# Layer 2 of a two-layer graph network: squares, adds, the last group's scores and the scaling of P in another order and on another engine

## The chip, the cores and the metric

The kernel runs on 1 core of one Trainium2 chip. The time is device microseconds of one execution, from start to end, the median of three runs. Each core has TensorE (PE, matrix products), VectorE (DVE), ScalarE (ACT), GpSimd (POOL) and SyncE (SP, which here issues DMA transfers). The engines run their own instruction streams and meet only at semaphores.

## What is computed

128 graphs of 64 nodes with 384 features go through two attention layers. The second, which the change touches, is this one, with `x` the output of the first:

```python
def _L1_gnn_ref(x, spatial_encoding, edge_encoding, Wq, Wk, Wv, bv, Wo, bo):
    scale = jnp.asarray(HIDDEN, x.dtype) ** (-0.5)
    q = (x @ Wq.T).reshape(b, n, NUM_HEADS, HEAD)          # 12 heads of 32
    k = (x @ Wk.T).reshape(b, n, NUM_HEADS, HEAD)
    v = (x @ Wv.T + bv).reshape(b, n, NUM_HEADS, HEAD)
    bias = (spatial_encoding + edge_encoding)[:, None]     # twice adj
    scores = jnp.einsum('bqhd,bkhd->bhqk', q, k) * scale + bias
    row_nonzero = jnp.any(scores != 0, axis=-1, keepdims=True)
    scores = jnp.where(row_nonzero, scores, -jnp.inf)
    p = jnp.nan_to_num(jax.nn.softmax(scores, axis=-1))
    out = jnp.einsum('bhqk,bkhd->bqhd', p, v).reshape(b, n, h)
    return out @ Wo.T + bo
...
x = _layernorm(x + _L1_gnn_ref(x, adj, adj, ...), axis=-1)
```

## The kernel before

The 8192 rows (nodes) are cut into 32 groups of 256, each of 2 tiles of 128 rows. Layer 1 takes the first 1386 us of the span, layer 2 the rest; layer 2 has one function `step(g, ...)` per engine, written out for groups 0 and 1, run in a hardware loop for g = 2 to 30, and written out again for g = 31 (no more groups), 32 (back half alone) and 33 (squares and norm alone). There is no planner: each engine's order is the order of the calls in its `step`. The three steps of a group overlap: in step g the front half (V, scores, softmax) works on group g, the back half (P^T, PV, output projection, y) on b = g - 1, and the late part (layer norm) on g - 2. Q and K of group g + 1 are made in step g as well.

Precision: the dense products are made of three matmuls each, high and low parts of both operands (`mm3`), so activations are split into `xt_hi`/`xt_lo` and `ctxt_hi`/`ctxt_lo`: ScalarE writes the high part, VectorE subtracts it for the low part.

The order on each engine in a loop step:

- TensorE: `values(g, 0)` (V of tile 0, 9 matmuls), `turn_p` of both tiles of b (12 transposes into the banks `two`, which are the same PSUM as the scores' `four`), `values(g, 1)`, `wait_for_pv` (copies of P^T done, V rows swapped and kept, ctx's low part read), `scores(g)` (96 small matmuls), `pv` (96), `qk(g + 1)` in three banks (54), `attn_out(b)` (18). `turn_p` waits for the scaled P of its tile and for y of the group before (which reads the same banks).
- ScalarE: `square` twice, `take_pt` twice (P^T out of PSUM), `xt_high` (behind both tiles of V), `ctxt_high` twice (behind PV), `keep_v` (four copies), `norm` twice, then `take_q` three times with `exp` of tile 0 and 1 between them.
- VectorE: `take_v` twice, `xt_low`, `ctxt_low(b, 0)`, `add_adj` twice (scores plus adj, PSUM to SBUF), `find_max` twice, `ctxt_low(b, 1)`, per tile `find_magnitude` and `invert_sum` (sum, reciprocal, mask), then `finish(b)`: y = projection + residual for both tiles, and the mean.
- GpSimd: `root(g - 2)` (three small operations behind the squares), `shift` of both tiles (score minus maximum, into P), `scale_p` of both tiles (P times the reciprocal of its sum).
- SyncE: loads of x^T, the residual and adj, four swaps of V rows, and the store of the normed group.

Lines of the trace (a helper's line may stand for several places): L1423 is `mm3`; L1461 the scores; L1469 the transposes of P; L1488 PV; L1543 `xt_high`; L1549 `take_q`; L1557 and L1558 `keep_v`; L1562 `exp`; L1567 `take_pt`; L1574 `ctxt_high`; L1580 `square`; L1587 `norm`; L1636 `xt_low`; L1645 `take_v`; L1655 `add_adj`; L1663 `find_max`; L1670 `find_magnitude`; L1676, L1679, L1682 the sum, reciprocal and mask of `invert_sum`; L1689 `ctxt_low`; L1699 to L1703 `finish`; L1746 `shift`; L1753 `scale_p`; L1758 to L1762 `root`. L953 is layer 1's own subtraction of the maximum, on VectorE.

Of the kernel before, what the change touches and what calls it, by code (L numbers as in the profile page):

```python
# [26 lines left out]
ALU = mybir.AluOpType  # L27
# [3 lines left out]
P = 128  # L31
GRAPHS, NODES, D = 128, 64, 384
TOKENS = GRAPHS * NODES
TILES = 2
# [4 lines left out]
H0, H1 = 8, 12  # L39
# [1276 lines left out]
def layer1(nc, block, sem, x2, x2T, adj, out, shared, last, free):  # L1316
# [5 lines left out]
    with ExitStack() as ctx:  # L1322
# [21 lines left out]
        score, prob, pt = (sb(f"b_{n}", [P, TILES, S]) for n in ("score", "p", "pt"))  # L1344
# [74 lines left out]
        def _(pe):  # L1419
# [88 lines left out]
            def step(g, front=True, back=True, more=True):  # L1508
                b = g - 1
                if front:  # L1510
                    values(g, 0)
                if back:
                    for t in range(TILES):
                        turn_p(b, t)
                if front:
                    values(g, 1)
                if back:
                    wait_for_pv(b)
                if front:
                    scores(g, back)  # L1520
                if back:
                    for t in range(TILES):
                        pv(b, t)
                if front and more:
                    for u in range(3):
                        qk(g + 1, u)
                if back:
                    for t in range(TILES):
                        attn_out(b, t, front)
# [3 lines left out]
            with pe.Fori(2, NG - 1) as g:  # L1533
                step(g)
# [4 lines left out]
        def _(act):  # L1539
# [54 lines left out]

            def step(g, front=True, back=True, late=True, more=True):
                b = g - 1
                if late:
                    for t in range(TILES):
                        square(g - 2, t)
                if back:  # L1600
                    for t in range(TILES):
                        take_pt(b, t)
                if front and more:
                    xt_high(g + 1)
                if back:
                    for r in range(2):
                        ctxt_high(b, r)
                if front:
                    for t in range(TILES):
                        keep_v(g, t)  # L1610
                if late:
                    norm(g - 2)
                if front and more:
                    take_q(g + 1, 0)
                if front:
                    exp(g, 0)
                if front and more:
                    take_q(g + 1, 1)
                if front:
                    exp(g, 1)  # L1620
                if front and more:
                    take_q(g + 1, 2)
# [10 lines left out]
        def _(dve):  # L1633
# [38 lines left out]
            def invert_sum(g, t):  # L1672
# [9 lines left out]
                dve.scalar_tensor_tensor(out=rden[:, t, :], in0=samax[:, t, :], scalar=0.0, in1=rden[:, t, :],  # L1682
                                         op0=ALU.is_gt, op1=ALU.mult).then_inc(rden_masked, 1)

            def ctxt_low(g, r):
                dve.wait_ge(ctxt_hi, 2 * g + r + 1)
                for low, high, k in CTX_ROWS[r]:
                    at = (k - r) * GROUP
                    i = dve.tensor_tensor(ctx_t[1][low:high, k, :], one[PV_BANK[r]][low:high, at:at + GROUP],  # L1689
                                          ctx_t[0][low:high, k, :].bitcast(F32), ALU.subtract)  # L1690
                i.then_inc(ctxt_lo, 1)
# [15 lines left out]

            def step(g, front=True, back=True, late=True, more=True):
                b = g - 1
                if front:  # L1710
                    for t in range(TILES):
                        take_v(g, t)
                if front and more:
                    xt_low(g + 1)
                if back:
                    ctxt_low(b, 0)
                if front:
                    for t in range(TILES):
                        add_adj(g, t)
                    for t in range(TILES):  # L1720
                        find_max(g, t)
                if back:
                    ctxt_low(b, 1)
                if front:
                    for t in range(TILES):
                        find_magnitude(g, t)
                        invert_sum(g, t)
                if back:
                    finish(b)

# [9 lines left out]
        def _(pool):  # L1740
# [5 lines left out]
                pool.tensor_tensor(p, s, smax[:, t, :].unsqueeze(2).broadcast_to([P, H1, NODES]),  # L1746
                                   ALU.subtract).then_inc(shifted, 1)

            def scale_p(g, t):

                s = prob[:, t, :].rearrange("p (h n) -> p h n", h=H1)
                pool.wait_ge(rden_masked, TILES * g + t + 1)
                pool.tensor_tensor(s, s, rden[:, t, :].unsqueeze(2).broadcast_to([P, H1, NODES]), ALU.mult).then_inc(p_scaled, 1)  # L1753

            def root(g):

                pool.wait_ge(sq_done, TILES * (g + 1))
# [6 lines left out]
            def step(g, front=True, back=True, late=True, more=True):  # L1764
                if front and not back:
                    last["gpsimd"]()
                if late:
                    root(g - 2)
                if front:
                    for t in range(TILES):  # L1770
                        shift(g, t)
                    for t in range(TILES):
                        scale_p(g, t)

            step(0, back=False, late=False)
            step(1, late=False)
# [87 lines left out]
```

## Time and profile before

| what | value |
|---|---|
| median of 3 runs | 1971.73 us (1971.13 to 1973.51) |
| the profiled execution | 1973.86 us |
| its span, first to last instruction | 1972.0 us |
| PE, PEld (weight loads) busy | 95%, 93% |
| DVE busy | 66% |
| ACT busy | 55% |
| POOL busy | 25% |
| granted TensorE clock, mean | 0.98 |

Busy shares are means over both layers. Starts in the rows below are microseconds from the start of the span; a row of the timeline is start, duration, engine, line, operation, output<-inputs, shapes, and in brackets the idle time of the engine before it and what ended it. Several like instructions are merged into one row with their count (x2, x96). Recorded ends of neighbours on one engine overlap a little, so distances are best read from start to start.

### The profile page before, as it was taken

Reading aid. Unit: us, or ns where it says so; the run is one execution under the profiler, and the core shown is the slowest. Engines: PE = TensorE matmul, PEld = TensorE weight load, DVE = VectorE, ACT = ScalarE, POOL = GpSimd, SP = SyncE. Lnnn points to the kernel's source line nnn. Section 1 sums busy time; section 2 is a strip of 40 time slices with the busy share of each in tenths; the row PEclk is TensorE's granted clock in tenths of the full one; section 3 lists DMA queues with packets and bytes.
Section 4 is the critical chain, followed back from the end, with each engine's and each line's share of the span. In section 5 each row is a group of like instructions: output and inputs, shape, how many; then the busy total and the mean of one; then the engine's idle time right before and its main releaser. Section 6 shows DMA issues by size and latency. Waiting matters only on the chain.

```text
span 1972.0 us, 58076 instructions
## 1 busy us (share of the span) xinstructions
PE 1870.0 (95%) x22160; PEld 1830.5 (93%) x22160; DVE 1291.8 (66%) x2507; ACT 1081.0 (55%) x2366; POOL 496.2 (25%) x616
## 2 busy tenths in 40 slices
PE   7699999999999999999999999988799999999996
PEld 6599999999999999999999999988789999999995
DVE  5566666666666666666666666654577777777775
ACT  4365455654556545655556555544456656565654
POOL 0111122121221112121131211211333344433343
PEclk8899999999999999999999999999899999999998
DMA  7534444444444444444444444334322233222231
GB/s 184 150 105 113 126 119 113 127 109 128 116 119 120 112 129 115 124 118 109 135 109 123 117 113 132 99 98 106 84 80 71 84 88 88 80 81 76 85 88 59
DMA packets 268682, 213.42 MB, mean 108 GB/s; under 512 B 142816, under 2 KB 251104, under 8 KB 268640
## 3 DMA queue, kind: packets, MB, share of 16 engines
q1 hardware_dynamic: 268640, 212.85, 39.6%
q8 instruction: 28, 0.46, 0.1%
q14 instruction: 14, 0.11, 0.0%
HBM read 120.33 MB, written 79.69 MB: 101 GB/s over the span
## 4 chain that ended last, share of the span: by engine, by line
PE 83%; ACT 5%; DVE 4%; DMA 3%; SPq 3%; issue 2%; POOL 0%; ACTq 0%; DVEq 0%; POOLq 0%
PE a_bank L446 29%; PE a_banks L446 28%; PE b_bank L1423 12%; PE b_banks L1423 5%; PE a_bank L495 2%; ACT b_pt L1567 2%; PE b_banks L1461 2%; PE b_bank L1488 2%; PE a_banks L515 2%; SPq L262 1%; PE b_banks L1469 1%; ACT b_unused L1580 1%; DMA a_work<-x_turned 1%; DMA x_turned<-a_work 0%; DMA a_work<-ctx_turned 0%
## 5 line engine op out<-in xcount | busy, mean ns | idle before, releaser
L446 PE MATMUL a_bank<-a_x1t_hi,a_w_hi 128*128 128x256 f32 x1152 | 328.2, 285 | 20.1 <-DVE a_x1t_lo L917 20.1
L446 PE MATMUL a_bank<-a_x1t_hi,a_w_lo 128*128 128x256 f32 x1152 | 324.7, 282 | 0.0
L446 PE MATMUL a_bank<-a_x1t_lo,a_w_hi 128*128 128x256 f32 x1152 | 324.6, 282 | 0.0
L734 ACT ACTIVATE a_work<-a_bank,a_b 128x256 f32<-128x256 f32 x384 | 160.2, 468 | 203.4 <-PE a_bank L446 202.9
L446 PE MATMUL a_banks<-a_w_hi,a_hid_hi 128*128 128x384 f32 x768 | 258.8, 337 | 0.6 <-DVE a_hid_lo L932 0.6
L446 PE MATMUL a_banks<-a_w_hi,a_hid_lo 128*128 128x384 f32 x768 | 258.2, 336 | 0.0
L446 PE MATMUL a_banks<-a_w_lo,a_hid_hi 128*128 128x384 f32 x768 | 258.2, 336 | 0.0
L932 DVE TENSOR_TENSOR a_hid_lo<-a_work,a_hid_hi 128x512 fp32r<-128x512 f32 x192 | 131.6, 698 | 191.1 <-ACT a_hid_hi L739 191.1
L446 PEld LDWEIGHTS a_bank<-a_x1t_hi,a_w_hi 128*128 128x128 f32 x1152 | 221.0, 192 | 22.9 <-DVE a_x1t_lo L917 21.0
L446 PEld LDWEIGHTS a_bank<-a_x1t_lo,a_w_hi 128*128 128x128 f32 x1152 | 221.6, 192 | 0.0
L446 PEld LDWEIGHTS a_bank<-a_x1t_hi,a_w_lo 128*128 128x128 f32 x1152 | 220.5, 191 | 0.0
L1253 POOL TENSOR_TENSOR a_ms<-a_ssq,eps_rms 128x2 f32<-128x2 f32 x64 | 12.5, 195 | 641.7 <-ACT a_work L744 641.7
L1746 POOL TENSOR_TENSOR b_p<-b_score,b_smax 128x768 f32<-128x768 f32 x64 | 93.1, 1475 | 232.0 <-DVE b_smax L1663 232.0
L446 PEld LDWEIGHTS a_banks<-a_w_hi,a_hid_hi 128*128 128x128 f32 x768 | 144.4, 188 | 1.0 <-DVE a_hid_lo L932 1.0
L446 PEld LDWEIGHTS a_banks<-a_w_hi,a_hid_lo 128*128 128x128 f32 x768 | 144.5, 188 | 0.0
L446 PEld LDWEIGHTS a_banks<-a_w_lo,a_hid_hi 128*128 128x128 f32 x768 | 144.3, 188 | 0.0
L721 ACT ACTIVATE a_x1t_hi<-a_work 128x768 fp32r<-128x768 f32 x32 | 27.1, 847 | 211.2 <-DMA a_work<-x_turned 211.2
L739 ACT ACTIVATE a_hid_hi<-a_work 128x512 fp32r<-128x512 f32 x192 | 121.5, 633 | 8.2
L1753 POOL TENSOR_TENSOR b_p<-b_p,b_rden 128x768 f32<-128x768 f32 x64 | 94.3, 1474 | 56.7 <-DVE b_rden L1682 56.7
L1253 POOL TENSOR_TENSOR a_ms<-a_ssq,eps_ln 128x2 f32<-128x2 f32 x32 | 6.5, 203 | 405.3 <-ACT a_work L744 405.3
L926 DVE TENSOR_TENSOR a_work<-a_banks,a_bv 128x384 f32<-128x384 f32 x64 | 35.6, 558 | 106.6 <-PE a_banks L446 106.4
L1580 ACT ACTIVATE b_unused<-b_y,b_nmean_c 128x384 f32<-128x384 f32 x64 | 38.9, 611 | 112.4 <-DVE b_nmean_c L1703 112.4
(172 smaller groups left out, 5615.2 us busy)
## 6 DMA issues: line engine op xcount, KB each, us to landing
a_work<-in_x SPq DMA_DIRECT2D x64, 384.0 KB, 3.3
p_turned<-a_work SPq DMA_DIRECT2D x256, 64.0 KB, 2.3
a_work<-p_turned SPq DMA_DIRECT2D x32, 512.0 KB, 3.3
xt_raw<-in_xT SPq DMA_DIRECT2D x32, 384.0 KB, 3.9
ctx_turned<-a_work SPq DMA_DIRECT2D x256, 48.0 KB, 1.7
a_work<-ctx_turned SPq DMA_DIRECT2D x32, 384.0 KB, 3.5
x_turned<-a_work SPq DMA_DIRECT2D x256, 48.0 KB, 1.7
a_work<-x_turned SPq DMA_DIRECT2D x32, 384.0 KB, 3.8
```

Source lines behind the costliest of these rows:

```text
L446: r = pe.matmul(out, lhs[a], rhs[b], start=first and n == 0, stop=last and n == 2)
L495: r = pe.matmul(PV_BANK[t][64 * s:64 * s + 64, h * 2 * VW:(h + 1) * 2 * VW].rearrange("p (r c) -> p r c", r=2), pt[:, t, s * 256 + h * 64: ...
L515: r = pe.matmul(s_banks[64 * s:64 * s + 64, i, at:at + n * NODES].rearrange("p (e n) -> p e n", e=n), q[row, m, nodes], k_t[row, m:m + n, ...
L734: r = act.activation(silu[:, p % 2, s * GROUP:(s + 1) * GROUP], A[p % 3][:, s * GROUP:(s + 1) * GROUP], ACT.Silu, bias=b1[:, m:m + 1])
L739: act.activation(hid[0][:, p % RING, :], silu[:, p % 2, :], ACT.Copy).then_inc(hid_hi, 1)
L932: dve.tensor_tensor(hid[1][:, p % RING, :], silu[:, p % 2, :], hid[0][:, p % RING, :].bitcast(F32), ALU.subtract).then_inc(hid_lo, 1)
L1423: r = pe.matmul(out, lhs[a], rhs[b], start=first and n == 0, stop=last and n == 2)
L1461: r = pe.matmul(four[64 * s:64 * s + 64, i, at:at + NODES], qk_t[row, k, nodes], qk_t[row, KT + k, nodes], start=True, stop=True, skip_gro ...
L1488: m = pe.matmul(one[PV_BANK[r]][32 * i:32 * i + 32, at:at + NODES], v_rows[rows, n, h * DH1:(h + 1) * DH1], pt[rows, t, h * P + 64 * s:h * ...
L1580: act.activation(unused[:, t, :], y[:, t, :], ACT.Square, bias=nmean_c[:, t:t + 1], scale=ROOT, accum_out=ssq[:, t:t + 1]).then_inc(sq_don ...
L1746: pool.tensor_tensor(p, s, smax[:, t, :].unsqueeze(2).broadcast_to([P, H1, NODES]), ALU.subtract).then_inc(shifted, 1)
L1753: pool.tensor_tensor(s, s, rden[:, t, :].unsqueeze(2).broadcast_to([P, H1, NODES]), ALU.mult).then_inc(p_scaled, 1)
```

## The change

All of it is in layer 2.

- ScalarE, loop step: the two squares of g - 2 move from the head of the step to behind `take_pt` and `xt_high`, ahead of `ctxt_high`; in the step that has no front half they come behind `ctxt_high`.
- VectorE, loop step: both `add_adj` move ahead of `ctxt_low(b, 0)`. `scale_p` moves from GpSimd to VectorE, behind `invert_sum` of its tile, with the same waits and the same semaphore.
- Group 31 (`front and not more`) gets an order of its own on TensorE, ScalarE and VectorE: TensorE makes its scores ahead of V's second tile and ahead of the transposes of group 30, with waits for y of the group before and for the adds; ScalarE does squares, norm and copies first and puts the exponentials between the halves of ctx's high part; VectorE takes the adds and maxima ahead of V's second tile.

```diff
--- before.py
+++ after.py
@@ -1509,14 +1509,19 @@
                 b = g - 1
                 if front:
                     values(g, 0)
+                if front and not more:
+                    pe.wait_ge(y_done, TILES * b)
+                    scores(g, back)
+                    values(g, 1)
+                    pe.wait_ge(biased, TILES * (g + 1))
                 if back:
                     for t in range(TILES):
                         turn_p(b, t)
-                if front:
+                if front and more:
                     values(g, 1)
                 if back:
                     wait_for_pv(b)
-                if front:
+                if front and more:
                     scores(g, back)
                 if back:
                     for t in range(TILES):
@@ -1594,17 +1599,32 @@
 
             def step(g, front=True, back=True, late=True, more=True):
                 b = g - 1
-                if late:
+                if front and not more:
                     for t in range(TILES):
                         square(g - 2, t)
+                    norm(g - 2)
+                    for t in range(TILES):
+                        take_pt(b, t)
+                    for t in range(TILES):
+                        exp(g, t)
+                        ctxt_high(b, t)
+                    for t in range(TILES):
+                        keep_v(g, t)
+                    return
                 if back:
                     for t in range(TILES):
                         take_pt(b, t)
                 if front and more:
                     xt_high(g + 1)
+                if front and late:
+                    for t in range(TILES):
+                        square(g - 2, t)
                 if back:
                     for r in range(2):
                         ctxt_high(b, r)
+                if late and not front:
+                    for t in range(TILES):
+                        square(g - 2, t)
                 if front:
                     for t in range(TILES):
                         keep_v(g, t)
@@ -1682,6 +1702,12 @@
                 dve.scalar_tensor_tensor(out=rden[:, t, :], in0=samax[:, t, :], scalar=0.0, in1=rden[:, t, :],
                                          op0=ALU.is_gt, op1=ALU.mult).then_inc(rden_masked, 1)
 
+            def scale_p(g, t):
+
+                s = prob[:, t, :].rearrange("p (h n) -> p h n", h=H1)
+                dve.wait_ge(rden_masked, TILES * g + t + 1)
+                dve.tensor_tensor(s, s, rden[:, t, :].unsqueeze(2).broadcast_to([P, H1, NODES]), ALU.mult).then_inc(p_scaled, 1)
+
             def ctxt_low(g, r):
                 dve.wait_ge(ctxt_hi, 2 * g + r + 1)
                 for low, high, k in CTX_ROWS[r]:
@@ -1707,17 +1733,35 @@
 
             def step(g, front=True, back=True, late=True, more=True):
                 b = g - 1
+                if front and not more:
+                    take_v(g, 0)
+                    for t in range(TILES):
+                        add_adj(g, t)
+                    for t in range(TILES):
+                        find_max(g, t)
+                    find_magnitude(g, 0)
+                    take_v(g, 1)
+                    invert_sum(g, 0)
+                    scale_p(g, 0)
+                    for r in range(2):
+                        ctxt_low(b, r)
+                    find_magnitude(g, 1)
+                    invert_sum(g, 1)
+                    scale_p(g, 1)
+                    finish(b)
+                    return
                 if front:
                     for t in range(TILES):
                         take_v(g, t)
                 if front and more:
                     xt_low(g + 1)
+                if front:
+                    for t in range(TILES):
+                        add_adj(g, t)
                 if back:
                     ctxt_low(b, 0)
                 if front:
                     for t in range(TILES):
-                        add_adj(g, t)
-                    for t in range(TILES):
                         find_max(g, t)
                 if back:
                     ctxt_low(b, 1)
@@ -1725,6 +1769,7 @@
                     for t in range(TILES):
                         find_magnitude(g, t)
                         invert_sum(g, t)
+                        scale_p(g, t)
                 if back:
                     finish(b)
 
@@ -1746,12 +1791,6 @@
                 pool.tensor_tensor(p, s, smax[:, t, :].unsqueeze(2).broadcast_to([P, H1, NODES]),
                                    ALU.subtract).then_inc(shifted, 1)
 
-            def scale_p(g, t):
-
-                s = prob[:, t, :].rearrange("p (h n) -> p h n", h=H1)
-                pool.wait_ge(rden_masked, TILES * g + t + 1)
-                pool.tensor_tensor(s, s, rden[:, t, :].unsqueeze(2).broadcast_to([P, H1, NODES]), ALU.mult).then_inc(p_scaled, 1)
-
             def root(g):
 
                 pool.wait_ge(sq_done, TILES * (g + 1))
@@ -1769,8 +1808,6 @@
                 if front:
                     for t in range(TILES):
                         shift(g, t)
-                    for t in range(TILES):
-                        scale_p(g, t)
 
             step(0, back=False, late=False)
             step(1, late=False)
```

## Rows read from the trace of the kernel before

**Rows 1.** Waits of layer 2: engine line <- releaser: us in total, times, longest us

```profile
PE b_banks L1461 <- ACT b_pt L1567: 21.3, 30, 0.8
```

**Rows 2.** Chain of work that ended last, one group: start us, us, what

```profile
1849.10 1.40 ACT b_pt L1567 x2
1850.50 0.43 issue
```

**Rows 3.** Timeline of TensorE in steps 26 and 27

```profile
1847.18 1.49 PE L1469 MATMUL b_banks<-ident,b_p 128*128 128x128 f32 x12
...
1849.89 0.34 PE L1423 MATMUL b_bank<-wv_lo,xt_hi 128*128 128x384 f32 x1
1850.93 1.25 PE L1461 MATMUL b_banks<-b_qk 32*64 32x64 f32 x96 [0.70 <-ACT b_pt L1567]
...
1864.36 0.34 PE L1423 MATMUL b_bank<-wv_lo,xt_hi 128*128 128x384 f32 x1
```

**Rows 4.** Timeline of VectorE: xt_low of groups 1 to 3, then one step

```profile
1414.15 0.96 DVE L1636 TENSOR_TENSOR xt_lo<-xt_raw,xt_hi 128x768 fp32r<-128x768 f32 x1 [0.38 <-ACT xt_hi L1543]
...
1430.84 0.96 DVE L1636 TENSOR_TENSOR xt_lo<-xt_raw,xt_hi 128x768 fp32r<-128x768 f32 x1 [0.34 <-ACT xt_hi L1543]
...
1449.93 0.96 DVE L1636 TENSOR_TENSOR xt_lo<-xt_raw,xt_hi 128x768 fp32r<-128x768 f32 x1 [0.34 <-ACT xt_hi L1543]
...
1851.26 0.96 DVE L1636 TENSOR_TENSOR xt_lo<-xt_raw,xt_hi 128x768 fp32r<-128x768 f32 x1 [0.34 <-ACT xt_hi L1543]
1854.04 0.75 DVE L1689 TENSOR_TENSOR b_ctxt_lo<-b_bank,b_ctxt_hi 128x256 fp32r<-128x256 f32 x2 [1.83 <-ACT b_ctxt_hi L1574]
1854.71 1.80 DVE L1655 TENSOR_TENSOR b_score<-b_banks,b_adj 128x768 f32<-128x768 f32 x2
1856.44 1.80 DVE L1663 TENSOR_REDUCE b_smax<-b_score 128x12 f32<-128x768 f32 x2
1858.27 0.87 DVE L1689 TENSOR_TENSOR b_ctxt_lo<-b_bank,b_ctxt_hi 64x256 fp32r<-64x256 f32 x2
1859.05 0.94 DVE L1670 TENSOR_REDUCE b_samax<-b_score 128x12 f32<-128x768 f32 x1
1859.93 0.95 DVE L1676 TENSOR_REDUCE b_psum<-b_p 128x12 f32<-128x768 f32 x1
...
1861.18 0.17 DVE L1682 SCALAR_TENSOR_TENSOR b_rden<-b_samax,b_rden 128x12 f32<-128x12 f32 x1
1861.26 0.94 DVE L1670 TENSOR_REDUCE b_samax<-b_score 128x12 f32<-128x768 f32 x1
...
1863.56 0.56 DVE L1699 SCALAR_TENSOR_TENSOR b_y<-b_banks,b_res 128x384 f32<-128x384 f32 x1
```

**Rows 5.** Timeline of ScalarE, the same step

```profile
1850.39 0.83 ACT L1543 ACTIVATE xt_hi<-xt_raw 128x768 fp32r<-128x768 f32 x1
1853.36 1.45 ACT L1574 ACTIVATE b_ctxt_hi<-b_bank 128x256 fp32r<-128x256 f32 x4 [2.14 <-PE b_bank L1488]
...
1856.21 1.31 ACT L1587 ACTIVATE b_normed<-b_y,b_ymean,b_rstd 128x384 f32<-128x384 f32 x2
1857.43 0.58 ACT L1549 ACTIVATE b_qk<-b_bank 128x512 f32<-128x512 f32 x1
```

**Rows 6.** Timeline of GpSimd, the same step

```profile
1857.54 2.91 POOL L1746 TENSOR_TENSOR b_p<-b_score,b_smax 128x768 f32<-128x768 f32 x2 [7.12 <-DVE b_smax L1663]
```

**Rows 7.** Timeline of TensorE in step 1, written out, without squares

```profile
1412.84 0.34 PE L1423 MATMUL b_bank<-wv_lo,xt_hi 128*128 128x384 f32 x1
1413.11 1.25 PE L1461 MATMUL b_banks<-b_qk 32*64 32x64 f32 x96
```

**Rows 8.** Line 953, layer 1: duration ns min/median/max, first and last start us

```profile
L953 DVE TENSOR_TENSOR a_work<-a_work,a_smax x64: 691/694/1329, 26.8 to 1280.6; 128x512 f32<-128x512 f32 x64
```

**Rows 9.** Timeline of TensorE, steps 31 and 32

```profile
1934.33 1.49 PE L1469 MATMUL b_banks<-ident,b_p 128*128 128x128 f32 x12
...
1955.29 1.29 PE L1488 MATMUL b_bank<-b_pt,b_v_rows 64*32 64x64 f32 x96 [1.95 <-ACT b_pt L1567]
```

## The prediction

> **What bounds the kernel now.** All edits lie in layer 2, so I read that layer alone. The table of waits names few stalls of TensorE there; the one that returns is 0.7 us ahead of the scores, put down to ScalarE's copy of P^T, 30 times [rows 1]. In the code the two squares stand right ahead of that copy; in the chain of waits of one group the two copies take 1.40 us, and 0.43 us of issue follow ahead of the scores [rows 2]. On TensorE itself the last matmul of V's second tile starts at 1849.89 and the scores at 1850.93, 1.04 us later [rows 3]. Group 1, which has no squares, shows what that step takes without a stall: 1412.84 to 1413.11, 0.27 us [rows 7]. So the stall costs 1.04 - 0.27 = 0.77 us a group. The period is the distance of two starts of xt_low: (1851.26 - 1449.93) / 23 = 17.45 us [rows 4]. TensorE without the stall would need 16.68.
>
> Then I read VectorE against it. From ctx's first low part (1854.04) to the first add of y (1863.56) it has no gap: each instruction starts as the last one ends [rows 4]. So the present ring is: y and its mean on VectorE, squares, copies of P^T, scores and PV, ctx's high part, VectorE's row of work, y again. TensorE is full, but the ring around VectorE is just as long.
>
> **The change part by part.** (a) Squares behind the copies and xt_high. They leave the way to the scores. Two of them cost about the 1.22 us of the equally large pair of norms (1856.21 to 1857.43) [rows 5]. The copies then end about 2.4 us after the transposes start (the second set of six transposes ends near 1.2, 0.4 for the signal, 0.8 for half the pair), and V's second tile has its last matmul 2.71 us after that start (1847.18 to 1849.89) [rows 3]. So the stall of 0.77 goes, if the five waits that follow in TensorE's queue (0.43 us behind the copy today [rows 2]) are passed meanwhile. Their new place is between xt_high (starts 1850.39, some 0.75) and ctx's high part, which waits for PV. Counted from V's last matmul (1849.89): xt_high at 0.50, squares 1.25 to 2.47, ctx's high part at 0.27 + 2.43 (1850.93 to 1853.36) = 2.70 [rows 3, 5]. They fit, with 0.2 to spare. GpSimd's three small operations come later, and norm behind the copies of V still finds them done.
>
> (b) Adds ahead of ctx's low part. VectorE no longer idles for ScalarE after xt_low (1851.26, 0.96 long): the adds follow it at once, since the scores are done by then. The low part (0.67 us, 1854.04 to 1854.71) goes behind them; its only near consumers, the third bank of the next Q/K and the output projection, come over 2 us later. Moved, at no price.
>
> (c) P scaled on VectorE. GpSimd's multiply goes (same width as its subtraction, 2.91 / 2 = 1.46 us [rows 6]); VectorE gets two of 128x768 with both inputs in SBUF. The nearest row is xt_low, 0.96 busy, 0.89 to the next start after the overlap seen between neighbours [rows 4]. The other row is layer 1's subtraction with the same broadcast, 0.69 for 512 columns at best, which gives 0.69 x 768 / 512 = 1.04 at most, and 1.33 at worst [rows 8]. I take 0.89; ends 0.85 and 1.04. Twice 0.89 plus 0.13 of waiting for each mask (0.21 in place of 0.08, an estimate from the mask's own length) is 2.0 us more on VectorE each group. This lies on the ring, because y is added behind it.
>
> VectorE's two-input multiply can collide with GpSimd. Layer 1's row shows the same instruction at 0.69 at best and 1.33 at worst [rows 8], though nothing about its own size varies. The Trainium skill (SBUF — State Buffer, Who interferes with whom) says that a VectorE instruction with two SBUF inputs and a GpSimd instruction that reads SBUF shut each other out for a whole instruction. By that rule the multiply is safe only where GpSimd rests; with it the sum would be the rival "collision" below, otherwise it stays as it is.
>
> (d) The new ring. From the start of xt_low: xt_low 0.89, adds 1.73 (1854.71 to 1856.44), low part 0.67, maxima 1.83 (to 1858.27), second low part 0.78, magnitude 0.88, sum to mask 1.25 (1859.93 to 1861.18), mask 0.21, multiply 0.89; then for tile 1 magnitude 0.88, 1.25, 0.21, 0.89; y 0.56 [rows 4]. That is 12.92. Then the wake of TensorE, an estimate of 0.15 (ends 0 and the 0.43 of rows 2), transposes and V to its last matmul 2.71 [rows 3], to xt_high 0.50, to xt_low 0.87 (1850.39 to 1851.26) [rows 4, 5]. Sum 17.15.
>
> Does the first sum find its exponential? By GpSimd: maxima start at 3.29, the subtraction follows 1.10 later as today (1856.44 to 1857.54), and 2.39 behind its start VectorE sums (to 1859.93) [rows 4, 6]: 3.29 + 1.10 + 2.39 = 6.78, just when VectorE is free (6.78). By ScalarE's queue, from V's last matmul: 0.27 + 2.43 to ctx's high part, 2.85 to norm, 1.22 to take_q, 0.58 to the exponential (its copy 0.5 to 0.58), 0.88 to the sum (2.39 less 1.46 of subtraction and 0.05 of signal), 8.2, less 1.37 for the start of xt_low: 6.85 [rows 3, 5]. That adds 0.05 to 0.07: **ring 17.20**, a saving of 0.25, not of 0.77. TensorE now waits for y ahead of the transposes: V's first tile ends its issue 13.42 us after the scores (1850.93 to 1864.36) [rows 3], y is some 0.5 later. The stall moves, and two thirds of it stay.
>
> (e) The start. Group 0 has no ring yet; tile 1 is ready 0.89 + 0.96 after where its mask was, against 1.46 on GpSimd: +0.4. From xt_low of group 1 to that of group 3 the kernel takes 35.78 now: 16.69 (no squares) and 19.09 [rows 4], 1.64 over the period, a stall of the first turn of the loop that stays. The new ring has no squares in it and gains nothing from their absence: 17.20 + 18.84 = 36.04, so +0.26.
>
> (f) The end. In group 31 the scores go ahead of V's second tile, and norm, squares and the rest are ordered anew. From the first transposes of group 31's turn (1934.33) to the last PV (1955.29) it is 20.96 now [rows 9]. New, from that same point: y of group 29 is through at 0.95, scores 1.1, adds 2.6 to 4.4, transposes 4.5, copies and PV at 7.0, PV 1.4, ctx's high part, one exponential and its second half 2.1, low part 1.0 to 11.7, projection 4.5 at TensorE's half clock as today, y 17.2, last transposes and copy with no squares ahead, PV 19.2. These are estimates from the same row lengths. Saved 1.75, between 0.5 and 3. From the last PV on nothing on the way to the store changes: the squares of group 30 now come behind ctx's high part, and norm still ends ahead of the last y.
>
> **Sum.** +0.4 +0.26, 27 periods x (-0.25) = -6.75, the stall of group 30 itself -0.77, the end -1.75: -8.6 us. Against the profiled execution's span of 1972.0 that is 1963.4; the profiled execution took 1973.9 in all and the median of the runs is 1971.7, so I forecast **1963.1**.
>
> **The rivals.** One: **TensorE bounds**. If VectorE's row were overlapped better than its starts show, the ring would fall under 16.68 and the whole stall goes: 28 x 0.77 = 21.6, the end 1.75, less 0.4: 1948.8. Against it: there is no gap in VectorE's row to give back, and the ring would have to be 0.5 shorter.
>
> Two: **the stall keeps its place or turns into one of the exponential**. If TensorE passes its six waits only after V's last matmul, the scores come at 0.27 + 0.35; ctx's high part, norm, take_q and the first exponential shift with them, and the ring is 17.20 + 0.25 to 0.35 = 17.45 to 17.55. Then 27 x 0 to +0.1 and the end: 1969 to 1973. For it: 0.43 us of issue today [rows 2]. Against it: transposes follow V with two waits and no gap.
>
> Three, slower: **ScalarE's queue becomes the ring**. From xt_high to the first sum it now holds, back to back, xt_high 0.75, squares 1.22, high part and copies of V 2.85, norm 1.22, take_q 0.55, exponential 0.88: 7.47 [rows 5, 6]. VectorE's way between the same two ends is 0.87 + 6.78 = 7.65. So the queue has 0.18 to spare; where its waits in the loop cost more than 0.18 together, every tenth goes on the period. Against the end's gain of 1.9 us it is slower than before from a ring of 17.52 on, that is from 0.18 + 0.37 = 0.55; at 0.8 the ring is 17.15 + 0.62 = 17.77 and the kernel 27 x 0.32 - 2 = +6.8: 1978.5.
>
> Four: **collision**. If the multiply of tile 0 met GpSimd's second subtraction it would wait, 0.64 by the spread of rows 8: period 17.84, 1980. Against it: the multiply comes at 8.24, the subtraction ends at 4.39 + 2.91 = 7.30, and both hang on the same maxima, so they keep their distance.
>
> **How the numbers follow.** Forecast (ring 17.05 to 17.35, 1959 to 1968) 0.50; TensorE bounds, or nearly (1945 to 1957), 0.15; no gain 0.22; ScalarE's queue 0.09; collision 0.04. The range 1952 to 1974 leaves out half of rival one and most of three and four, some 0.18. This kernel can be told from no change at about 0.2%, 4 us. Faster: 0.48 + 0.15 = 0.63; the same: 0.22 and rests of the forecast and of rival three, 0.27; slower: 0.10.
>
> **What would show it.** In the changed profile: the wait of the scores for the copy gone, and a wait of L1469 for b_y of about 0.5 us in its place, 29 times; xt_low to xt_low 17.2; VectorE without a gap from xt_low to y; the multiply 0.96 long; ScalarE's squares between xt_hi and ctxt_hi; the first exponential within 0.1 us behind take_q or the subtraction. A period of 16.7 and no wait of L1469 would make rival one right; a gap ahead of b_psum, rivals two or three, by whether V's last matmul to the scores is over 0.3 or ScalarE's queue is full.

## The result, and the profile after

The changed kernel takes 1958.9 us, the median of four runs (1957.0 to 1962.4), against 1972.5 of the kernel before beside it (1971.1 to 1973.5). The ratio is 0.9934 with a 95% interval of 0.9916 to 0.9951: faster by 13.6 us, 0.66%. The forecast was 1963.1, in a range of 1952 to 1974.

The profiled execution took 1957.6, with a span of 1955.8. Its page, busy time of the engines:

```profile
span 1955.8 us, 58047 instructions
...
PE 1871.5 (96%) x22160; PEld 1829.6 (94%) x22160; DVE 1339.6 (68%) x2571; ACT 1084.0 (55%) x2366; POOL 402.7 (21%) x552
```

64 instructions went from GpSimd to VectorE. GpSimd is busy 93.5 us less, VectorE 47.8 more; 64 multiplies of 0.957 would be 61 more. Some 10 of the missing 13 are the mean of y, which is 0.3 shorter in each group now (last section); the rest was not traced.

The table of waits of layer 2, the lines that answer to [rows 1] (engine line <- releaser: us in total, times, longest us):

```profile
ACT b_pt L1572 <- PE b_banks L1469: 162.7, 32, 6.5
...
PEld b_banks L1469 <- DVE b_y L1725: 15.0, 28, 0.6
...
PEld b_banks L1461 <- issue: 7.7, 30, 0.4
...
PE b_banks L1469 <- DVE b_y L1725: 6.3, 27, 0.2
```

The wait of the scores for the copy of P^T is no longer there. ScalarE's copy now waits for TensorE, in place of the other way round. In return the transposes (L1469) wait for VectorE's y in 28 groups, 0.54 us each by the weight loads (PEld): the stall has moved, as forecast.

One period on TensorE, as [rows 3] (timeline: start, duration):

```profile
1834.56 0.34 PE L1423 MATMUL b_bank<-wv_lo,xt_hi 128*128 128x384 f32 x1
1835.13 1.53 PE L1469 MATMUL b_banks<-ident,b_p 128*128 128x128 f32 x12 [0.23 <-DVE b_y L1725]
...
1837.89 0.34 PE L1423 MATMUL b_bank<-wv_lo,xt_hi 128*128 128x384 f32 x1
1838.16 1.25 PE L1461 MATMUL b_banks<-b_qk 32*64 32x64 f32 x96
```

From V's last matmul to the scores it is 0.27 us, where it was 1.04. From V's first tile to the transposes it is 0.57, where a start follows a start in 0.17.

VectorE, as [rows 4]:

```profile
1834.52 0.55 DVE L1725 SCALAR_TENSOR_TENSOR b_y<-b_banks,b_res 128x384 f32<-128x384 f32 x1
1834.99 0.08 DVE L1725 DVE_READ_ACCUMULATOR b_y<-b_banks,b_res 128x1 f32 x1
...
1839.14 0.96 DVE L1656 TENSOR_TENSOR xt_lo<-xt_raw,xt_hi 128x768 fp32r<-128x768 f32 x1 [0.23 <-ACT xt_hi L1548]
1840.02 1.82 DVE L1675 TENSOR_TENSOR b_score<-b_banks,b_adj 128x768 f32<-128x768 f32 x2
1841.75 0.74 DVE L1715 TENSOR_TENSOR b_ctxt_lo<-b_bank,b_ctxt_hi 128x256 fp32r<-128x256 f32 x2
1842.41 1.79 DVE L1683 TENSOR_REDUCE b_smax<-b_score 128x12 f32<-128x768 f32 x2
...
1845.02 0.94 DVE L1690 TENSOR_REDUCE b_samax<-b_score 128x12 f32<-128x768 f32 x1
1846.01 0.95 DVE L1696 TENSOR_REDUCE b_psum<-b_p 128x12 f32<-128x768 f32 x1
...
1847.47 0.96 DVE L1709 TENSOR_TENSOR b_p<-b_p,b_rden 128x768 f32<-128x768 f32 x1
1848.34 0.95 DVE L1690 TENSOR_REDUCE b_samax<-b_score 128x12 f32<-128x768 f32 x1
...
1850.65 0.96 DVE L1709 TENSOR_TENSOR b_p<-b_p,b_rden 128x768 f32<-128x768 f32 x1
1851.53 0.55 DVE L1725 SCALAR_TENSOR_TENSOR b_y<-b_banks,b_res 128x384 f32<-128x384 f32 x1
```

From xt_low to y there is one place where VectorE doesn't start on the heels of itself: magnitude to sum is 0.99 here, 0.88 in [rows 4]. ScalarE in the same step, as [rows 5]:

```profile
1838.27 0.84 ACT L1548 ACTIVATE xt_hi<-xt_raw 128x768 fp32r<-128x768 f32 x1 [0.61 <-PE b_bank L1423]
1839.02 0.60 ACT L1585 ACTIVATE b_unused<-b_y,b_nmean_c 128x384 f32<-128x384 f32 x1
...
1840.59 1.45 ACT L1579 ACTIVATE b_ctxt_hi<-b_bank 128x256 fp32r<-128x256 f32 x4 [0.28 <-PE b_bank L1488]
...
1843.45 1.31 ACT L1592 ACTIVATE b_normed<-b_y,b_ymean,b_rstd 128x384 f32<-128x384 f32 x2
1844.67 0.57 ACT L1554 ACTIVATE b_qk<-b_bank 128x512 f32<-128x512 f32 x1
1845.15 0.83 ACT L1567 ACTIVATE b_p<-b_p 128x768 f32<-128x768 f32 x1
```

The squares lie between xt_high and ctx's high part with 0.28 to spare. From that high part to the first exponential ScalarE has no gap.

Where the time of the profiled executions went, by the starts of xt_low:

| stretch | before | after | difference | forecast |
|---|---|---|---|---|
| layer 1, to xt_low of group 1 (first) | 1397.44 | 1392.96 | -4.48 | 0 |
| first to second | 16.71 | 17.84 | +1.13 | +0.4 |
| second to fourth | 35.78 | 37.14 | +1.36 | +0.26 |
| fourth to last, 27 periods | 471.13 | 459.25 | -11.88 | -6.75 |
| last to the end of the span | 50.94 | 48.61 | -2.33 | -2.52 |
| sum | 1972.0 | 1955.8 | -16.2 | -8.6 |

(What the prediction calls xt_low of group 1, 2 and so on is this table's second, third and so on; the first one is written in step 0.)

Layer 1 is the same code. In the profiled executions of the kernels below, which share it too, it ends (first xt_low) anywhere from 1391.0 to 1396.1, so its -4.5 here is taken as variation between executions. Layer 2 alone gave 11.7 us in these two traces, by a period of 17.01 in place of 17.45.

### The profile page after: what moved, and what is told of

It is laid out like the page before. It is cut to its first block, busy times and chain, and to the rows that moved or that the text cites. A ratio compares the mean times of both kernels' runs of the same rounds, so it can differ in the third digit from the quotient of the medians.

```text
span 1955.8 us, 58047 instructions
## 1 busy us (share of the span) xinstructions
PE 1871.5 (96%) x22160; PEld 1829.6 (94%) x22160; DVE 1339.6 (68%) x2571; ACT 1084.0 (55%) x2366; POOL 402.7 (21%) x552
## 4 chain that ended last, share of the span: by engine, by line
PE 73%; DVE 9%; ACT 7%; issue 5%; DMA 2%; SPq 2%; POOL 0%; ACTq 0%; DVEq 0%; POOLq 0%
PE a_bank L446 30%; PE a_banks L446 28%; PE b_bank L1423 4%; DVE b_psum L1696 3%; PE b_banks L1469 2%; PE a_bank L495 2%; PE a_banks L515 2%; ACT b_normed L1592 2%; PE b_banks L1461 2%; PE b_bank L1488 2%; DVE b_samax L1690 1%; ACT b_p L1567 1%; SPq L262 1%; ACT b_v_rows L1562 1%; DVE b_y L1725 1%
## 5 line engine op out<-in xcount | busy, mean ns | idle before, releaser
L1572 ACT ACTIVATE b_pt<-b_banks 128x768 f32<-128x768 f32 x64 | 48.6, 809 | 162.8 <-PE b_banks L1469 162.7
L1423 PE MATMUL b_bank<-xt_hi,wq_hi 128*128 128x256 f32 x288 | 85.5, 297 | 11.0 <-DVE xt_lo L1656 11.0
```

The source lines that it names most:

```text
L1423: r = pe.matmul(out, lhs[a], rhs[b], start=first and n == 0, stop=last and n == 2)
L1572: act.activation(pt[:, t, :], two[t][:, 0:S], ACT.Copy).then_inc(pt_done, 1)
```

## The experiments

A ring is a closed chain of waits: each engine in it waits for the one before, and the first for the last, so that one way round sets the time of a group. Two theories stood against each other. **Theory one**: a ring through VectorE sets the period; the old one ran through squares and copies, the new one through VectorE's row with both multiplies in it. **The rivals**: ScalarE's queue sets it, or VectorE has room and the multiply is free. In the table, "period" is the distance of the starts of xt_low from the fourth to the last, divided by 27.

| kernel | us, median | ratio to before, 95% | period |
|---|---|---|---|
| before | 1970.6 to 1972.5 | 1 | 17.45 |
| the change | 1958.9 | 0.9934 (0.9916 to 0.9951) | 17.01 |
| squares_alone | 1945.3 | 0.9870 (0.9848 to 0.9891) | 16.66 |
| adds_alone | 1945.3 | 0.9863 (0.9844 to 0.9883) | 16.57 |
| multiply_alone | 2019.0 | 1.0243 (1.0215 to 1.0271) | 19.01 |
| adds_back | 1993.1 | 1.0106 (1.0085 to 1.0126) | 18.16 |
| multiply_split | 1945.4 | 0.9863 (0.9847 to 0.9880) | 16.55 |
| norm_behind_exp | 1954.6 | 0.9909 (0.9893 to 0.9926) | 16.89 |
| old_last_step | 1957.3 | 0.9932 (0.9912 to 0.9953) | 17.00 |
| squares_and_adds | 1942.0 | 0.9850 (0.9835 to 0.9866) | 16.55 |
| all_but_multiply | 1940.6 | 0.9847 (0.9829 to 0.9866) | 16.55 |
| all_but_multiply_again | 1940.6 | 0.9850 (0.9834 to 0.9866) | 16.57 |

Each kernel ran beside its own runs of the kernel before, so kernels are best compared by their ratios. The medians are of two runs (adds_alone, multiply_alone, adds_back) to six, the period is that of one trace. Theory one's expectations held for the periods to within 0.2 us. Of its times three were 3 to 9 us too high (squares_alone, adds_alone, all_but_multiply) and one 1.4 too low (multiply_split), as said at each.

**Squares alone**, on the kernel before:

```diff
@@ ScalarE, step
-                if late:
-                    for t in range(TILES):
-                        square(g - 2, t)
                 if back:
                     for t in range(TILES):
                         take_pt(b, t)
                 if front and more:
                     xt_high(g + 1)
+                if front and late:
+                    for t in range(TILES):
+                        square(g - 2, t)
```

(In the step without a front half they come behind ctx's high part, as in the change.)

> Kernel before with the squares' new place in the loop as its only edit. Theory one (the old ring ran through the squares, the new one through VectorE with two multiplies more in it): without the multiplies VectorE's y is early enough, the stall of 0.77 us ahead of the scores goes in full, the distance from xt_low to xt_low falls from 17.45 to 16.7, and the kernel takes about 1972 - 28 x 0.77 = 1950. Rival (ScalarE's queue sets the ring, wherever the multiply is): the distance stays at 17.0 as in the whole change, and the time is about 1960.

Measured 1945.3, period 16.66. The whole stall goes, and this one edit is worth 25 us, nearly twice the whole change. The time is 5 us under the expected 1950, which counted the stall alone; by the traces the loop's first turn gave 0.8 more (18.33 between the third and fourth xt_low, for 19.09) and the end 2.4 (48.57 for 50.94). The transposes in it (timeline of TensorE and of GpSimd):

```profile
1840.80 1.58 PE L1469 MATMUL b_banks<-ident,b_p 128*128 128x128 f32 x12
```

```profile
1839.90 1.48 POOL L1756 TENSOR_TENSOR b_p<-b_p,b_rden 128x768 f32<-128x768 f32 x1 [0.72 <-DVE b_rden L1685]
```

GpSimd's second multiply ends at 1841.38, just as the second six transposes are due (1840.80 + 0.6). The weight load of the seventh starts at 1841.50, 0.27 behind that of the sixth, where the step is 0.11. The twelve take 1.58, where they take 1.47 below: 0.1 us a group still hangs on GpSimd.

**Adds alone**, on the kernel before:

```diff
@@ VectorE, step
+                if front:
+                    for t in range(TILES):
+                        add_adj(g, t)
                 if back:
                     ctxt_low(b, 0)
                 if front:
                     for t in range(TILES):
-                        add_adj(g, t)
-                    for t in range(TILES):
                         find_max(g, t)
```

> Kernel before with the adds ahead of ctx's low part as its only edit; the squares stay ahead of the copies of P^T. Theory one (one ring, squares included): VectorE starts its row about 1.6 us earlier against the scores, y and its mean come earlier by as much, so the squares are through before the transposes are, and the stall of 0.77 us goes here too: distance of xt_low 16.6 to 16.8, kernel 1948 to 1952. Rival (the stall hangs on the order of squares and copies alone): the distance stays 17.45 and the time at 1971.

Measured 1945.3, period 16.57, both a little under what was expected. The squares still stand ahead of the copies of P^T, and yet the stall is gone. Their order alone was not its cause: it took that order and the lateness of y, which they need. Either move opens the old ring by itself.

**The multiply alone**, on the kernel before:

```diff
@@ VectorE, step
                     for t in range(TILES):
                         find_magnitude(g, t)
                         invert_sum(g, t)
+                        scale_p(g, t)
@@ GpSimd, step
                     for t in range(TILES):
                         shift(g, t)
-                    for t in range(TILES):
-                        scale_p(g, t)
```

> Kernel before with P scaled on VectorE as its only edit. Theory one (VectorE's row of work from ctx's low part to y lies on the old ring too): two multiplies of 0.87 and two waits for the mask of 0.13 lengthen it by 2.0, the mean of y is no longer held up by GpSimd (0.3 less), the distance from xt_low to xt_low becomes 19.1 to 19.2, the kernel about 2018 to 2022. Rival (VectorE has room, since it is busy 13 of 17.4 us): under 0.3 us a group, 1972 to 1980.

Measured 2019.0, period 19.01 (0.1 under the expected): 1.56 us more a group. VectorE was busy 336 of 450 us in the loop of the kernel before, and still there was no room at this place.

**The adds put back**, on the changed kernel: the diff of adds_alone, the other way round.

> Changed kernel with the adds behind ctx's low part again, in the loop. Theory one: VectorE's row of 12.03 us now starts at ctx's high part; wake 0.06, transposes and V 2.76, to the scores 0.27, to ctx's high part 2.43, its first half 0.68, the row 12.03: distance 18.2, kernel about 1992. Rival (ScalarE's queue sets the ring): distance 17.0 to 17.2, under 1966.

Measured 1993.1, period 18.16, where 18.2 was worked out. The table of waits, us 1460 to 1900:

```profile
PEld b_banks L1469 <- DVE b_y L1725: 42.5, 25, 1.7
...
DVE b_ctxt_lo L1715 <- ACT b_ctxt_hi L1579: 28.3, 24, 1.2
```

VectorE waits for ctx's high part 1.2 us a group again, and TensorE waits for y 1.7. Without the adds the rest of the change makes the kernel slower than before.

**All but the multiply**, on the changed kernel: `scale_p` back on GpSimd, squares, adds and group 31 as changed.

```diff
@@ VectorE, step (and the same in the order of group 31)
                         invert_sum(g, t)
-                        scale_p(g, t)
@@ GpSimd, step
                     for t in range(TILES):
                         shift(g, t)
+                    for t in range(TILES):
+                        scale_p(g, t)
```

> Changed kernel with P scaled on GpSimd as before; squares, adds and the last group stay changed. Theory one: VectorE's row is 2.0 us shorter, P of the second tile is ready 0.5 us before TensorE wants it, TensorE waits for nothing in the loop, the distance is 16.65 to 16.7, and the kernel takes about 1959 - 27 x 0.33 = 1950 or a little less. Rival (ScalarE's queue sets the ring, or GpSimd's multiply of 1.47 us takes over): 17.0 or more, 1958 to 1965.

Measured 1940.6, period 16.55, the fastest kernel of this study: 30 us under the one before. Under the change it is by some 17, by the ratios and by layer 2 of the two traces (562.8 and 545.4 us). That is 9 us more than was expected, where only the loop's periods were counted: they give 12.3 us, the start and the loop's first turn 4.1, the end 1.0. Its transposes follow V without a wait and take 1.47; the ring on VectorE is shorter than TensorE's own work:

```profile
1837.60 1.47 PE L1469 MATMUL b_banks<-ident,b_p 128*128 128x128 f32 x12
1840.56 1.25 PE L1461 MATMUL b_banks<-b_qk 32*64 32x64 f32 x96
...
1854.15 1.47 PE L1469 MATMUL b_banks<-ident,b_p 128*128 128x128 f32 x12
```

**The multiply split**: tile 0 on VectorE, tile 1 on GpSimd.

```diff
@@ VectorE, step (in the order of group 31 the call for tile 1 is dropped)
                         invert_sum(g, t)
-                        scale_p(g, t)
+                        if t == 0:
+                            scale_p(g, t)
@@ GpSimd, step
                     for t in range(TILES):
                         shift(g, t)
+                    scale_p(g, 1)
```

> Changed kernel with P of tile 0 scaled on VectorE and P of tile 1 on GpSimd. Theory one: the row up to y falls by one multiply and its wait, 1.0 us, which is more than the 0.46 us by which the changed kernel's distance (17.01) lies over that of the kernel with both on GpSimd (16.55); so 16.55 to 16.6 and 1941 to 1944. Rival (each multiply on VectorE costs the same wherever it stands): half the loss stays, 16.78, 1949.

Measured 1945.4, period 16.55. One multiply on VectorE costs nothing in the loop, the second 0.46 us a group. A price by the instruction, 0.23 each, is ruled out: the cost begins where the ring passes TensorE's 16.55. The time is 1.4 us above the expected range. Against all_but_multiply it is 3.2 us more by the ratios and 3.4 by layer 2 of the traces, and 2.6 of these lie in the first interval of xt_low, 18.84 in place of 16.28: the second six transposes there wait 2.53 us for GpSimd's P of tile 1, and V behind them runs at a lower clock (see (e) below).

**Norm behind the first exponential**, on the changed kernel:

```diff
@@ ScalarE, step
-                if late:
+                if late and not front:
                     norm(g - 2)
                 if front and more:
                     take_q(g + 1, 0)
                 if front:
                     exp(g, 0)
+                if late and front:
+                    norm(g - 2)
```

> Changed kernel with the two norms (1.22 us) behind the first exponential on ScalarE. In the changed kernel VectorE's first sum starts 0.12 us after VectorE is free, and ScalarE runs without a gap from ctx's high part to that exponential. If ScalarE's queue is the last link of the ring, the exponential comes earlier, the wait of 0.12 goes and nothing more, because VectorE's own row is next: distance 16.89, 3 to 4 us less, 1955. Rival (ScalarE's queue alone sets the ring and VectorE is not part of it): 1.2 us less a group, down to TensorE's 16.55, 1946. Rival (the wait is GpSimd's subtraction): unchanged at 17.01.

Measured 1954.6, period 16.89, as worked out. The exponential now waits for GpSimd, ends in time, and VectorE's sum follows its magnitude in 0.88 (timelines of ScalarE and VectorE):

```profile
1845.03 0.85 ACT L1567 ACTIVATE b_p<-b_p 128x768 f32<-128x768 f32 x1 [0.97 <-POOL b_p L1793]
```

```profile
1845.03 0.94 DVE L1692 TENSOR_REDUCE b_samax<-b_score 128x12 f32<-128x768 f32 x1
1845.91 0.95 DVE L1698 TENSOR_REDUCE b_psum<-b_p 128x12 f32<-128x768 f32 x1
```

Of 1.22 us taken off ScalarE's queue 0.12 a group come back. The changed kernel's ring ran by scores, PV and ScalarE's queue from ctx's high part to the exponential, and VectorE's own row stood 0.12 behind that way.

**The old order of group 31**, on the changed kernel: the three branches `if front and not more` are left out and group 31 runs like the loop's steps.

> Changed kernel with group 31 in the order of the loop, as before. By the forecast the new order of group 31 is worth 1.75 us (0.5 to 3), so this one takes 1959 + 1.75 = 1960.7, with the distance of xt_low in the loop unchanged at 17.01. Rival (the waits for y and for the adds that the new order puts into TensorE's queue eat what it gives): same as the change, or faster by up to 1 us.

Measured 1957.3 against 1958.9, each with its own runs of before, the ratios 0.9932 and 0.9934: no difference to be told, and not the 1.75 forecast. From the last xt_low to the end the traces give 49.4 and 48.6, which speaks for 0.8. The same question with P on GpSimd, both kernels on the same chip: squares_and_adds is the kernel before with the diffs of squares_alone and adds_alone, all_but_multiply_again is all_but_multiply once more.

> Kernel before with both moves of the loop (squares, adds) and nothing else: P on GpSimd, group 31 in the old order. Distance of xt_low 16.55, as with both moves and the new order of group 31. If that new order is worth the forecast 1.75 us, this kernel is that much slower than the one beside it; by the two traces with the multiply on VectorE (49.4 and 48.6 from the last xt_low to the end) it is 0.8. Rival: no difference, both within 0.5.

> The changed kernel with P scaled on GpSimd once more, beside the kernel above on the same chip: 1940 to 1941, 1 to 2 us under it if the order of group 31 is worth what was forecast.

Measured 1942.0 (1941.3 to 1945.0) and 1940.6 (1939.4 to 1945.6): 1.4 us in favour of the new order, with ranges that overlap. The stretch from the last xt_low to the end is 47.1 with the old order and 47.3 and 47.6 in the two traces with the new one, so the traces do not put a gain there. They differ more plainly from the last matmul of group 31's first V tile to the last PV: with P on VectorE 20.86 us in the old order and 19.84 in the new, with P on GpSimd 18.37 and 18.61 to 18.83. So by single traces the new order gives some 1 us to the changed kernel and nothing once P is back on GpSimd; the medians can tell neither.

## Why the prediction was right, and where its terms were off

**What bounds, and the ring.** The step from the stall to a ring through VectorE is shown: the adds alone, which leave the squares where they were, remove the stall too. Three kernels with other rings came out at the period worked out ahead for them to within 0.2 us (18.16 for 18.2, 16.89 for 16.89, 19.01 for 19.1 to 19.2), the first two of them from links measured in the changed kernel; a fourth, multiply_split, came out at TensorE's own 16.55, for 16.55 to 16.6.

**The sum.** In the traces layer 2 gave 11.7 us for the 8.6 of the forecast. The loop's gain was put 5.1 us too small and the loss at the start 1.8 too small, the end was off by 0.2; so the total is nearer than its largest term, by errors that offset each other in part.

**(a) and (b), squares and adds.** Both did what was said. But they were costed as if both were needed. Each alone takes the period to 16.57 or 16.66, and "moved, at no price" hid that the adds are worth 1.15 us a group once the multiply is on VectorE (18.16 less 17.01).

**(c), the multiply.** 0.957 us, 0.87 to 0.88 to the next start, for the 0.89 taken. Nothing collided: its shortest and longest are 0.957 and 0.961. With both on VectorE the change gives away 0.46 us a group against GpSimd.

**(d), the new ring, 17.20 forecast and 17.01 measured.** Again by its links. VectorE's row from xt_low to y, 12.92 forecast, is 1839.14 to 1851.53 and 0.55 = 12.94, 0.12 of it the wait for the exponential (forecast 0.05 to 0.07), so the row itself was put 0.1 too long. The wake of TensorE, an estimate of 0.15, is 1835.07 to 1835.13 = 0.06. Transposes and V 2.76 for 2.71. From V's last matmul to xt_high it is 0.38 for 0.50, then 0.87 as forecast. The 0.50 was read from a step in which ScalarE was still in its copies of P^T (second copy until 1850.50 [rows 2]) when V was ready; the row showed ScalarE's queue, not the latency from V. Three links were put 0.31 too long together, two 0.11 to 0.12 too short: 0.19 us a period. That is 5.1 us over 27 periods, the largest miss of the sum.

**TensorE's own bound, 16.68 forecast and 16.55 measured.** The 17.45 of before held a second stall beside the one of 0.77: the transposes of tile 1 waited about 0.1 for GpSimd's P, as squares_alone still shows. It was in the timeline of the kernel before, where twelve transposes took 1.49 in one step [rows 3] and 1.56 in the next (1.57 in the median of the loop), and I did not ask why:

```profile
1864.53 1.56 PE L1469 MATMUL b_banks<-ident,b_p 128*128 128x128 f32 x12
```

**(e), the start, +0.66 forecast and +2.49 measured.** The second six transposes wait 2.00 us for the multiply, where they waited 1.21:

```profile
1406.27 0.88 PE L1469 MATMUL b_banks<-ident,b_p 128*128 128x128 f32 x6 [2.00 <-DVE b_p L1709]
```

The multiply was not later than before in these two traces: P of tile 1 is ready 13.25 us behind the first xt_low in both, and TensorE came to it 0.8 earlier. (In five other traces with P on GpSimd it is ready at 12.8 to 13.0, in the four others with both tiles on VectorE at 13.4 to 13.7, so that the forecast 0.4 has the right size.) The whole 1.13 of the first interval lies behind these transposes, where V's second tile runs at a lower granted clock. These are windows of the changed kernel (length, then PE, PEld, DVE, ACT and POOL busy with their counts, then the granted clock, 1.00 being 2.4 GHz and 0.50 being 1.2, DMA share and GB/s):

```profile
1406.00:1410.00 4.00, 3.73 (x31) 3.30 (x39) 0.81 (x3) 0.89 (x2) 0.00 (x0) 0.66 0.12 44
...
1430.00:1433.00 3.00, 2.25 (x33) 2.17 (x34) 1.42 (x4) 1.69 (x6) 0.16 (x1) 0.69 0.03 5
```

and about the same places before:

```profile
1407.00:1410.00 3.00, 2.54 (x18) 2.27 (x16) 2.56 (x5) 1.03 (x2) 2.26 (x2) 1.00 0.53 105
...
1430.00:1433.00 3.00, 2.13 (x167) 1.91 (x167) 1.46 (x2) 0.81 (x2) 0.00 (x1) 1.00 0.02 5
```

The starts of V's nine matmuls span 2.42 us here and 1.47 before. All twelve traces agree: behind waits of 1.21 to 1.47 us at this place the nine span 1.47 to 1.48 (eight traces), behind waits of 1.97 to 2.53 they span 2.12 to 2.71 (the change, norm_behind_exp, multiply_alone, multiply_split). The price of a wait at the start was taken as its length alone.

In the loop's first turn, the other part of the 2.49, the clock is low again behind a stall of 1.92 us in PV (1.44 before), which the prediction took as unchanged:

```profile
1430.74 0.46 PE L1488 MATMUL b_bank<-b_pt,b_v_rows 64*32 64x64 f32 x25 [1.92 <-issue]
```

The stall's length alone does not explain the clock: squares_and_adds has the same 1.92 there and a clock of 1.00 over the 4 us that follow, where the changed kernel has 0.57. Why is open.

**(f), the end, -2.52 forecast with the last stall and -2.33 measured.** The total is near, its parts are less so. From the last matmul of group 31's first V tile to the last PV it is 21.14 us before and 19.84 in the changed kernel, 1.30 less, where the new order was put at 1.75. The changed kernel with the old order has 20.86 there, so some 1.0 of it is the order's. In the prediction norm "still ends ahead of the last y", and so it does. Ahead of the first of the two y it is close: norm ends 0.34 us before it in the changed kernel (1946.15 and 1946.49). In all_but_multiply norm is what releases it, at the end of 3.17 us of idling:

```profile
1929.23 0.56 DVE L1719 SCALAR_TENSOR_TENSOR b_y<-b_banks,b_res 128x384 f32<-128x384 f32 x1 [3.17 <-ACT b_normed L1592]
```

But norm costs little there: y starts 0.76 behind the ninth matmul of its projection (1928.47), and 0.65 behind it in the changed kernel (1945.84). The last y waits for TensorE in both.

**The rivals.** TensorE bounds: not in the change (17.01 against 16.55), but at once when a multiply leaves VectorE. No gain from the issue of six waits: refuted, scores follow V in 0.27 in the loop as in group 1. ScalarE's queue: the full queue from xt_high on, as this rival has it, was not the limit, since ScalarE idles 0.28 ahead of ctx's high part; what costs 0.12 us a group is the way by PV into ScalarE that (d) had at 0.05 to 0.07, and not the 0.5 that would have mattered. Collision: did not occur; that VectorE and GpSimd can hold each other up in this kernel is shown in the last section.

## What to carry to other kernels

Follow the ring, not the stalled engine. Here TensorE's stall named ScalarE's copy, but the ring was opened at either of two links, the squares or the adds, and the squares' move alone did nearly twice what the whole change does. Before work is moved to a busy engine, ask what stands behind it there: two multiplies on VectorE stood ahead of y, which the transposes wait for, and gave back some 17 of 30 us, though they took GpSimd's slower instruction out. A latency read from a row holds only if the waiting engine was idle in that row.

## What the runs showed of the hardware

The mean of y, a VectorE instruction on two columns, took 0.47 us in the median before, and ended as GpSimd's multiply did (1846.19 and 1.47 = 1847.66; the mean 1847.22 and 0.47 = 1847.69). In all_but_multiply, where the multiply is still on GpSimd but y comes later against it, the mean takes 0.21 and again ends with it (1835.54 and 1.48 = 1837.02; 1836.83 and 0.21 = 1837.04). With the multiply off GpSimd it takes 0.17 in all 32 groups (line, engine, operation, count: shortest, median and longest in ns), before and after:

```profile
L1702 DVE TENSOR_SCALAR b_nmean<-b_ysum x32: 169/474/590, 1426.7 to 1964.9; 128x2 f32<-128x2 f32 x32
```

```profile
L1728 DVE TENSOR_SCALAR b_nmean<-b_ysum x32: 169/170/171, 1424.1 to 1948.7; 128x2 f32<-128x2 f32 x32
```

The Trainium skill (SBUF — State Buffer, Who interferes with whom) states that a VectorE instruction in a mode that uses both its ports, which `tensor_scalar` can enter, contends with GpSimd, and that whichever issues first keeps the shared ports for its whole instruction. The trace agrees here, with 0.30 us a group; which mode the mean of y runs in it does not show. By the rows it lay on the old ring, ahead of the squares; what it was worth there was not measured apart. VectorE's multiply met no GpSimd instruction and took 0.957 us each time.

The first stretch of layer 2 shows how a wait of TensorE costs more than its length: behind 2.00 us of waiting in place of 1.21 the granted clock over 4 us (1406 to 1410) is 0.66, where it was 1.00 before (1410 to 1414), and the nine matmuls there take 1 us longer.
